# An adapter block whose token maxima change PSUM banks: from the pair of banks of the main maxima to a ring of three, in four units of two heads

## The chip, the cores and the metric

The kernel runs on one core of one Trainium2 chip. The metric is the time of one execution on the device, in microseconds (us); smaller is better. A profiled execution gives a trace of every instruction on the engines: PE (TensorE matmul) and PEld (its weight load), DVE (VectorE), ACT (ScalarE), POOL (GpSimd) and SP (which issues the transfers).

## The reference, cut to what matters

Three blocks follow one another on x (8 batches, 256 tokens, width 160) and a context (8 batches, 512 rows, width 96): a cross attention with an adapter branch, then a self attention, then a second cross attention with a feed-forward at the end. The change lies in the first. The context splits into 508 keys `enc` and 4 tokens `ca`:

```
query = x @ Wq;  hs = mha(query, enc @ Wk, enc @ Wv)            # 8 heads of 20
ca_q1 = einsum('btc,th->bch', ca, Wq_ca)[:, indices, :]         # 96 distinct rows out of 4 tokens
ca_hs1 = mha(ca_q1, x, x)                                       # 96 queries over 256 rows of x
ca_hs2 = mha(ca_hs1 @ Wq, ca @ Wk_ca, ca @ Wv_ca)               # over 4 keys
out = (hs + ca_hs2) @ Wout + b_out + x
```

The softmax of `ca_hs1` needs, for each of 96 queries and each of 8 heads, the maximum of its scores over the 256 rows of x. These are "the tokens' maxima over x".

## The kernel before, in words

The first block is one program of numbered **slots**, g = 0 to 38. A pair of heads p (four pairs in a batch, 32 in all) enters at slot p and passes on: its q and k are projected in slot p, its maxima found in slot p+2, turned ("mt") in slot p+3, its scores computed in slot p+4 and its output weighed in slot p+5 ("weigh", in four groups). A slot has two steps, 0 and 1; each engine walks the same list `items(g)` in the same order, so the order of work on every engine is written out by hand and each engine is first in, first out.

The work of a whole batch is spread over the slots by offsets: `add(step, what, offset)` puts a unit for batch b into slot 4b + offset. A period is thus four slots. I name them for batch b: slot **A** is 4b+1, **B** is 4b+2, **C** is 4b+3, **D** is 4b+4 (the slot in which the next batch begins its "rows").

PSUM has eight banks: two for the main maxima (`max_bank`), two for scores (`score_bank`), one for the weighed sums (`pv_bank`), and three `shared` ones, used as a ring. The class `Order` lists all the units that go through the ring in the order of the slots; unit number n uses bank n mod 3. TensorE fills a bank after `claim(key)`, which waits until the unit three places before has been read: by VectorE (semaphore `emptied`), or for "mt", "d1" and "e1" by ScalarE (`turned`). VectorE increments `emptied` in the order of the list, so a claim also waits for every earlier read of VectorE.

In `max_bank` two kinds of units alternate. `find_max` (L2091) does two matmuls per step of a pair, and VectorE reduces them (L1881). `top` (L2137) does four matmuls for four heads of the token scores, and VectorE reduces them (L1893) into `top_q`; there are two for a batch, at the ends of slots A and B. `find_max` of step 0 waits for `top_read` of the preceding `top`, and `top` waits for `max_read`. After both, "mq" (slot C, step 1) turns the maxima.

The units of the ring that the text names: "e3" (adapter branch, read by L1807 and L1809), "ot" (attention output turned, filled by L1965 and L1966, read by ScalarE and then L1775 and L1776), "out" 0 and 1 (output projection L1977, read by L1782), "x" (next batch's x turned, L1942 and L1943, read by ScalarE and then L1762, L1763), "q" and "k" (L2081, read by ScalarE and then L1754, L1758), "qw" (L2163), "ctx" (next batch's context turned, L1949, read by ScalarE L1666 and then VectorE L1767), "d1" (L1993), "v" (L1958), "rows" (L1985).

Of the kernel before, what the change touches and what calls it, by code (L numbers as in the profile page):

```python
# [15 lines left out]
AX = mybir.AxisListType  # L16
# [1273 lines left out]
def adapter(nc, x, x_dram, const, ident_tile, shapes, ctx_dram, l0, self_weights):  # L1290
# [33 lines left out]
    def items(g):  # L1324

        out = []

        def add(step, what, offset, *n):
            if (b := batch(g, offset)) is not None:
                out.append((step, (what, b, *n)))  # L1330

        add(0, "s2", 8)
        add(0, "v", 4, 1)
        add(0, "p2", 8)
        add(0, "e3", 9)
        add(0, "out", 10, 0)
        add(0, "out", 10, 1)
        if (b := batch(g, -1)):
            out.append((0, ("ctx", b)))
        add(0, "d1", 7)  # L1340
        if (p := pair(g, MT)) is not None:
            out.append((0, ("mt", p)))
        add(0, "ot", 9)
        if (b := batch(g, -2)):
            out.append((0, ("x", b)))
        if (p := pair(g, WEIGH)) is not None:
            out += [(0, ("weigh", p, group)) for group in (0, 1)]
        if (p := pair(g, 0)) is not None:
            out += [(1, ("q", p)), (1, ("k", p))]
        if g < 4:  # L1350
            out += [(1, key) for key in ([("w", 0), ("w", 1), ("ct",)], [("qk", n) for n in range(4)],
                                         [("g2",), ("vt",)], [("vo",)])[g]]
        add(1, "xv", 4)
        add(1, "qs", 4, 0)
        add(1, "qs", 5, 1)
        if (p := pair(g, WEIGH)) is not None:
            out += [(1, ("weigh", p, group)) for group in (2, 3)]
        add(1, "top", 1, 0)
        add(1, "top", 2, 1)
        add(1, "rows", 0)  # L1360
        add(1, "mq", 3)
        add(1, "d2", 7)
        add(1, "v", 3, 0)
        add(1, "e1", 8)
        add(1, "qw", 6)
        return out

    ELSEWHERE = ("weigh", "top", "qs", "s2", "p2", "xv")
    pre = [("ctx", 0), ("x", 0), ("wt",)]
    order = Order(pre + [key for g in range(SLOTS) for _, key in items(g) if key[0] not in ELSEWHERE], ("mt", "d1", "e1"))  # L1370

# [9 lines left out]
    with stack:  # L1381
# [127 lines left out]
        x_bo_ready = sem("x_bo_ready")  # L1509
        r_hi = sem("r_hi")  # L1510
        cm_ready = sem("cm_ready")
        top_filled = sem("top_filled")
        top_read = sem("top_read")
        q_scored = sem("q_scored")
        q_exped = sem("q_exped")
        q_split = sem("q_split")
# [216 lines left out]
        def _(dve):  # L1733
# [143 lines left out]
            def slot(g):  # L1877
                for step in range(ROUNDS):
                    if (p := pair(g, MAX)) is not None:
                        dve.wait_ge(max_filled, p * ROUNDS + step + 1)  # L1880
                        nc.vector.reduce_max(maxima[:, p % 2, step, :, 0], max_bank[:, :].rearrange("p (j k) -> p j k", j=2)[:, :, 0:KEYS],  # L1881
                                             AX.X).then_inc(max_read, 1)
                    for at, key in items(g):
                        if at != step or key[0] in ("weigh", "mt", "d1", "e1", "qs", "xv", "s2"):
                            continue
                        if key[0] in SETUP:
                            set_up(key)
                        elif key[0] == "p2":
                            second_softmax(key[1])
                        elif key[0] == "top":  # L1890
                            _, b, n = key
                            dve.wait_ge(top_filled, b * 2 + n + 1)
                            nc.vector.reduce_max(top_q[:, CDIM + 4 * n:CDIM + 4 * n + 4],  # L1893
                                                 max_bank[0:CDIM, :].rearrange("p (h k) -> p h k", h=4), AX.X).then_inc(top_read, 1)
                        else:
                            extra(key)
                if (p := pair(g, WEIGH)) is not None:
                    dve.wait_ge(pv_done, p + 1)
                    groups = pv_bank[:, 0:4 * AV]
                    nc.vector.reciprocal(recip[:, :], groups.rearrange("p (g d) -> p g d", d=AV)[:, :, AD]).then_inc(recip_ready, 1)  # L1900
                    dve.wait_ge(recip_ready, p + 1)
                    head = p % APAIRS * 2
                    out = attn[p // APAIRS % 2][:, :, head * AD:(head + 2) * AD].rearrange("p t (h d) -> p h t d", h=2)
                    nc.vector.tensor_tensor(out, groups.rearrange("p (h t d) -> p h t d", h=2, t=QT)[:, :, :, 0:AD],
                                            recip[:, :].rearrange("p (h t) -> p h t", h=2)[:, :, :, None].to_broadcast([P, 2, QT, AD]),
                                            ALU.mult).then_inc(attn_ready, 1)
# [13 lines left out]
        def _(pe):  # L1920
# [8 lines left out]
            def extra(key):  # L1929
# [48 lines left out]
                elif what == "rows":  # L1978
                    bank_ = claim(key)
                    if b == 0:  # L1980
                        pe.wait_ge(diag_ready, 3)
                    passes = [(diag_h[:, 0], x_h[j][:, 0, :]), (diag_h[:, 0], x_l[j][:, :]), (diag_l[:, :, :], x_h[j][:, 0, :]),
                              (diag_h[:, 1], x_h[j][:, 1, :])]
                    for n, (lhs, rhs) in enumerate(passes):
                        mm = nc.tensor.matmul(bank_[:, 0:SEQ], lhs.rearrange("p r c -> p (r c)"), rhs, start=n == 0, stop=n == 3)  # L1985
                elif what == "mq":
                    pe.wait_ge(top_read, b * 2 + 2)
                    bank_ = claim(key)
                    mm = nc.tensor.transpose(bank_[:, 0:CDIM], top_q[:, :], ident[0:CDIM, 0:CDIM])
                elif what == "d1":  # L1990
                    pe.wait_ge(emptied, order.read(("qw", b)))
                    bank_ = claim(key)
                    nc.tensor.transpose(bank_[:, 0:CDIM], hs1[:, 0:HA], ident[0:CDIM, 0:CDIM])  # L1993
                    mm = nc.tensor.transpose(bank_[0:HB, CDIM:2 * CDIM], hs1[:, HA:HID], ident[0:CDIM, 0:CDIM])
                elif what == "d2":
                    pe.wait_ge(turned, order.turned(("d1", b)))
                    bank_ = claim(key)
                    out = bank_[0:CDIM, 0:HT]
                    nc.tensor.matmul(out, hs1_t[:, 0, :], g2[:, 0, b, :], start=True, stop=False)
                    mm = nc.tensor.matmul(out, hs1_t[0:HB, 1, :], g2[0:HB, 1, b, :], start=False, stop=True)  # L2000
                elif what == "e1":
                    pe.wait_ge(p2_ready, b + 1)
                    bank_ = claim(key)
                    mm = nc.tensor.transpose(bank_[0:HT, 0:CDIM], p2n[:, :, :].rearrange("p h t -> p (h t)"), ident[0:CDIM, 0:CDIM])
                elif what == "e3":
                    pe.wait_ge(turned, order.turned(("e1", b)))
                    bank_ = claim(key)
                    rows = slice(b % 4 * HT, (b % 4 + 1) * HT)
                    mm = nc.tensor.matmul(bank_[0:CDIM, 0:HID], p2_t[rows, :], vo[rows, b // 4, :], start=True, stop=True)
# [74 lines left out]
            def find_max(g, step, p):  # L2084
                at = p % KEPT
                if step == 0:
                    pe.wait_ge(emptied, order.read(("k", p)))
                    after(pe, top_read, extra_fills(g, 1))
                after(pe, max_read, p * ROUNDS + step)
                for j, half in enumerate(HALF):  # L2090
                    mm = nc.tensor.matmul(max_bank[:, j * 512:j * 512 + KEYS], q_s[half, at, step * P:(step + 1) * P],  # L2091
                                          k_s[half, at, 0:KEYS], start=True, stop=True)
                mm.then_inc(max_filled, 1)
# [31 lines left out]
                if group == 3:  # L2125
                    mm.then_inc(pv_done, 1)

            def top(g, b, n):

                j = b % 2  # L2130
                if n == 0:
                    pe.wait_ge(emptied, order.read(("rows", b)))
                    pe.wait_ge(cm_ready, b + 1)
                after(pe, top_read, b * 2 + n)
                after(pe, max_read, issued(g, MAX))
                for h in range(4):
                    mm = nc.tensor.matmul(max_bank[0:CDIM, h * SEQ:(h + 1) * SEQ], c_m[j][0:3 * HT, 4 * n + h, :],  # L2137
                                          r_s[j][0:3 * HT, :], start=True, stop=True)
                mm.then_inc(top_filled, 1)

            def token_scores(g, b, t):

# [24 lines left out]
            def slot(g):  # L2167
                for step in range(ROUNDS):
# [4 lines left out]
                    for at, key in items(g):  # L2173
# [4 lines left out]
                        elif key[0] in ("q", "k"):  # L2178
                            project(key)
                        elif key[0] == "top":  # L2180
                            top(g, key[1], key[2])
                        elif key[0] == "qs":
                            token_scores(g, key[1], key[2])
                        elif key[0] == "qw":
# [54 lines left out]
```

## Time and profile before

| | us |
|---|---|
| three runs of the kernel | 1373.13, 1379.3, 1382.82; median 1379.3 |
| the profiled execution | 1376.87 |
| its span, from first to last instruction | 1375.0 |
| TensorE busy in it | 1272.2 (93%) |
| VectorE busy in it | 963.3 (70%) |

The profiled execution is 2.4 us below the median and 1.9 us longer than its span. The first block takes the first 307 us of the span, about a fifth. Busy time of TensorE is an upper bound of its real work, since matmuls are pipelined and their ends are modelled. The granted TensorE clock is given as a share of full speed (2.4 GHz); 0.50 is 1.2 GHz.

### The profile page before, as it was taken

Reading aid. Unit: us, or ns where it says so; the run is one execution under the profiler, and the core shown is the slowest. Engines: PE = TensorE matmul, PEld = TensorE weight load, DVE = VectorE, ACT = ScalarE, POOL = GpSimd, SP = SyncE. Lnnn points to the kernel's source line nnn. Section 1 sums busy time; section 2 is a strip of 40 time slices with the busy share of each in tenths; the row PEclk is TensorE's granted clock in tenths of the full one; section 3 lists DMA queues with packets and bytes.
Section 4 is the critical chain, followed back from the end, with each engine's and each line's share of the span. In section 5 each row is a group of like instructions: output and inputs, shape, how many; then the busy total and the mean of one; then the engine's idle time right before and its main releaser. Section 6 shows DMA issues by size and latency. Waiting matters only on the chain. (4 is left out here: it accounts for less than half of the span.)

```text
span 1375.0 us, 39629 instructions
## 1 busy us (share of the span) xinstructions
PE 1272.2 (93%) x16812; PEld 1084.5 (79%) x16812; DVE 963.3 (70%) x1758; ACT 779.5 (57%) x1420; POOL 810.6 (59%) x866
## 2 busy tenths in 40 slices
PE   4889999976999999999889999999999999999597
PEld 3677777755989989899757888888888888887597
DVE  4677887734777777777457767686867676765584
ACT  2366666644656665665346656565656665655364
POOL 2278887657645655555426656566656565667364
PEclk9999999957999999999969999999999999999798
DMA  6001110002000000000010000000010000000000
GB/s 133 21 11 50 50 35 2 2 7 65 2 2 2 2 3 2 2 2 2 1 42 8 2 8 2 8 2 8 1 49 2 2 2 2 2 2 2 13 15 25
DMA packets 31992, 20.40 MB, mean 15 GB/s; under 512 B 21415, under 2 KB 30347, under 8 KB 31819
## 3 DMA queue, kind: packets, MB, share of 16 engines
q1 hardware_dynamic: 31819, 17.88, 5.2%
q8 instruction: 135, 2.21, 0.7%
q14 instruction: 38, 0.31, 0.1%
HBM read 16.56 MB, written 1.31 MB: 13 GB/s over the span
## 5 line engine op out<-in xcount | busy, mean ns | idle before, releaser
L530 POOL TENSOR_TENSOR cross_probs_l<-cross_probs 128x1024 f16<-128x1024 f32 x160 | 302.6, 1893 | 54.6 <-ACT cross_probs L614 54.6
L614 ACT ACTIVATE cross_probs<-cross_score 128x1024 f32<-128x1024 f32 x160 | 163.9, 1024 | 189.4 <-PE cross_score L844 189.4
L698 DVE TENSOR_REDUCE cross_top<-cross_max 128x2 f32<-128x1024 f32 x160 | 195.7, 1223 | 63.6 <-PE cross_max L818 63.6
L1618 POOL TENSOR_TENSOR ad_probs_l<-ad_probs 128x1024 f16<-128x1024 f32 x64 | 120.8, 1893 | 91.2 <-ACT ad_probs L1692 90.8
L530 POOL TENSOR_TENSOR self_probs_l<-self_probs 128x1024 f16<-128x1024 f32 x80 | 151.4, 1892 | 1.2 <-ACT self_probs L614 1.2
L864 PEld LDWEIGHTS cross_pv<-cross_v_h,cross_probs 128*128 128x128 bf16 x1280 | 117.1, 98 | 38.0 <-issue 26.8
L614 ACT ACTIVATE self_probs<-self_score 128x1024 f32<-128x1024 f32 x80 | 81.9, 1024 | 110.9 <-PE self_score L844 110.8
L864 PE MATMUL cross_pv<-cross_v_h,cross_probs 128*128 128x65 bf16 x1280 | 135.7, 196 | 6.1 <-POOL cross_probs_l L530 5.3
L865 PE MATMUL cross_pv<-cross_v_l,cross_probs 128*128 128x64 f16 x1280 | 134.4, 194 | 0.0
L866 PE MATMUL cross_pv<-cross_v_h,cross_probs_l 128*128 128x65 bf16 x1280 | 134.0, 194 | 0.0
L844 PE MATMUL cross_score<-cross_qk_h 64*128 64x256 f32 x640 | 120.5, 373 | 0.0
L865 PEld LDWEIGHTS cross_pv<-cross_v_l,cross_probs 128*128 128x128 bf16 x1280 | 118.8, 99 | 0.2
L866 PEld LDWEIGHTS cross_pv<-cross_v_h,cross_probs_l 128*128 128x128 f16 x1280 | 118.7, 99 | 0.0
L684 DVE TENSOR_TENSOR cross_qk_l<-cross_shared,cross_qk_h 128x256 fp32r<-128x256 f32 (+1 forms) x160 | 88.0, 553 | 32.8 <-ACT cross_qk_h L599 32.6
L698 DVE TENSOR_REDUCE self_top<-self_max 128x4 f32<-128x1024 f32 x80 | 97.7, 1222 | 17.9 <-PE self_max L823 17.7
L511 POOL CAST cross_maxima<-cross_top 128x4 bf16<-128x4 f32 x80 | 16.0, 200 | 151.3 <-DVE cross_top L698 151.3
L511 POOL CAST self_maxima<-self_top 128x4 bf16<-128x4 f32 x80 | 16.1, 202 | 136.1 <-DVE self_top L698 136.0
L1692 ACT ACTIVATE ad_probs<-ad_score 128x1024 f32<-128x1024 f32 x64 | 65.5, 1024 | 52.5 <-PE ad_score L2103 51.8
L599 ACT CAST cross_qk_h<-cross_shared 128x256 fp32r<-128x256 f32 (+1 forms) x160 | 76.1, 477 | 26.7 <-PE cross_shared L800 23.9
L844 PE MATMUL cross_score<-cross_qk_l,cross_qk_h 64*128 64x256 f32 x640 | 90.3, 279 | 0.0
L844 PE MATMUL cross_score<-cross_qk_h,cross_qk_l 64*128 64x256 f32 x640 | 90.2, 278 | 0.0
L684 DVE TENSOR_TENSOR self_qk_l<-self_shared,self_qk_h 128x512 fp32r<-128x512 f32 x80 | 55.2, 690 | 42.8 <-ACT self_qk_h L599 42.6
(438 smaller groups left out, 4792.4 us busy)
## 6 DMA issues: line engine op xcount, KB each, us to landing
ad_ctx_rows<-in_ctx SPq DMA_DIRECT2D x8, 192.0 KB, 2.8
cross_ctx_rows<-in_ctx SPq DMA_DIRECT2D x8, 192.0 KB, 2.6
sw_raw<-in_L_xattn_wq SPq DMA_DIRECT2D x2, 640.0 KB, 6.1
sw_raw<-in_L_xattn_wk SPq DMA_DIRECT2D x2, 640.0 KB, 4.8
sw_raw<-in_L_xattn_wv SPq DMA_DIRECT2D x2, 640.0 KB, 5.2
cw_raw<-in_L_xattn_wq SPq DMA_DIRECT2D x2, 640.0 KB, 4.2
lr_raw<-in_L_xattn_w_ff SPq DMA_DIRECT2D x2, 640.0 KB
out<-x_rows SPq DMA_DIRECT2D x8, 160.0 KB, 1.9
```

The source lines that it names most:

```text
L511: nc.gpsimd.tensor_copy(maxima[:, p % 2, :, :, 0], top[:, p % 2, :, :]).then_inc(max_hi, 1)
L530: nc.gpsimd.tensor_tensor(probs_l[:, n % PR, :, :].rearrange("p j k -> p (j k)"), whole, whole.bitcast(BF16)[:, 1::2], ALU.subtract).then_ ...
L599: nc.scalar.copy(qk_h[:, kept(parity, s), at:at + width], shared[ring.bank(kind, key)][:, 0:width]).then_inc(qk_hi, 1)
L614: nc.scalar.activation(probs[:, n % PR, :, :].rearrange("p j k -> p (j k)"), score_bank[:, :], ACT.Exp, scale=SCALE).then_inc(exped, 1)
L684: nc.vector.tensor_tensor(qk_l[:, kept(parity, s), at:at + width], shared[ring.bank(kind, key)][:, 0:width], qk_h[:, kept(parity, s), at:a ...
L698: nc.vector.reduce_max(out, scores, AX.X).then_inc(max_read, 1)
L844: mm = nc.tensor.matmul(score_bank[:, j * 512 + c * SEQ:j * 512 + (c + 1) * SEQ], ks[half, at, keys], qs[half, at, 0:SEQ], start=False, st ...
L864: nc.tensor.matmul(pv_bank[:, at:at + DV], hi, v_h[parity][:, c, head, :], start=c == 0, stop=False)
L865: nc.tensor.matmul(pv_bank[:, at:at + DH], hi, v_l[parity][:, c, head, :], start=False, stop=False)
L866: mm = nc.tensor.matmul(pv_bank[:, at:at + DV], lo, v_h[parity][:, c, head, :], start=False, stop=last)
L1618: nc.gpsimd.tensor_tensor(probs_l[:, n % PR, :, :].rearrange("p j k -> p (j k)"), whole, whole.bitcast(BF16)[:, 1::2], ALU.subtract).then_ ...
L1692: nc.scalar.activation(probs[:, n % PR, :, :].rearrange("p j k -> p (j k)"), score_bank[:, :], ACT.Exp, scale=SCALE).then_inc(exped, 1)
```

## The change: what it does

The tokens' maxima no longer use `max_bank`. They become four units of two heads each (n = 0 to 3), which go through the ring of three shared banks: n = 0 in slot A, step 0, behind "ot"; n = 1 in slot A, step 1, where `top` 0 stood; n = 2 in slot B, step 1, where `top` 1 stood; n = 3 in slot C, step 0, behind "mt". I call them T0 to T3. The two semaphores `top_filled` and `top_read` go; `find_max` no longer waits for a token unit, and the token units no longer wait for `max_read`. They claim a ring bank instead. "mq" waits for the read of T3.

```diff
         add(0, "ot", 9)
+        add(0, "top", 1, 0)
+        add(0, "top", 3, 3)
         if (b := batch(g, -2)):
             out.append((0, ("x", b)))
...
-        add(1, "top", 1, 0)
-        add(1, "top", 2, 1)
+        add(1, "top", 1, 1)
+        add(1, "top", 2, 2)
...
-    ELSEWHERE = ("weigh", "top", "qs", "s2", "p2", "xv")
+    ELSEWHERE = ("weigh", "qs", "s2", "p2", "xv")
...
# VectorE
-                            dve.wait_ge(top_filled, b * 2 + n + 1)
-                            nc.vector.reduce_max(top_q[:, CDIM + 4 * n:CDIM + 4 * n + 4],
-                                                 max_bank[0:CDIM, :].rearrange("p (h k) -> p h k", h=4), AX.X).then_inc(top_read, 1)
+                            dve.wait_ge(filled, order.filled(key))
+                            nc.vector.reduce_max(top_q[:, CDIM + 2 * n:CDIM + 2 * n + 2],
+                                                 shared[order.bank(key)][0:CDIM, :].rearrange("p (h k) -> p h k", h=2), AX.X).then_inc(emptied, 1)
...
# TensorE, "mq"
-                    pe.wait_ge(top_read, b * 2 + 2)
+                    pe.wait_ge(emptied, order.read(("top", b, 3)))
...
# TensorE, find_max
                     pe.wait_ge(emptied, order.read(("k", p)))
-                    after(pe, top_read, extra_fills(g, 1))
                 after(pe, max_read, p * ROUNDS + step)
...
# TensorE, top
-            def top(g, b, n):
+            def top(b, n):
...
-                after(pe, top_read, b * 2 + n)
-                after(pe, max_read, issued(g, MAX))
-                for h in range(4):
-                    mm = nc.tensor.matmul(max_bank[0:CDIM, h * SEQ:(h + 1) * SEQ], c_m[j][0:3 * HT, 4 * n + h, :],
+                bank_ = claim(("top", b, n))
+                for h in two:
+                    mm = nc.tensor.matmul(bank_[0:CDIM, h * SEQ:(h + 1) * SEQ], c_m[j][0:3 * HT, 2 * n + h, :],
                                           r_s[j][0:3 * HT, :], start=True, stop=True)
-                mm.then_inc(top_filled, 1)
+                mm.then_inc(filled, 1)
```

## Rows read from the trace of the kernel before

**Rows 1.** The page: busy time, share and instructions of each engine.

```profile
PE 1272.2 (93%) x16812; PEld 1084.5 (79%) x16812; DVE 963.3 (70%) x1758; ACT 779.5 (57%) x1420; POOL 810.6 (59%) x866
```

**Rows 2.** Windows, slot A to A: length; busy PE, PEld, DVE, ACT, POOL; clock.

```profile
94.39:125.48 31.09, 28.18 (x388) 23.63 (x388) 24.90 (x46) 21.75 (x42) 26.70 (x16) 0.95 0.18 49
...
217.06:248.41 31.35, 28.29 (x388) 23.61 (x387) 24.90 (x46) 20.85 (x41) 24.12 (x15) 0.95 0.01 2
```

**Rows 3.** Windows, slots A, B, C, D of batch 4.

```profile
155.87:163.72 7.85, 6.41 (x83) 4.85 (x83) 7.17 (x14) 5.79 (x12) 7.85 (x7) 1.00 0.37 125
163.72:172.74 9.02, 8.78 (x137) 7.88 (x138) 6.41 (x11) 5.36 (x8) 7.23 (x5) 0.81 0.06 22
172.74:179.58 6.84, 6.54 (x86) 5.49 (x87) 5.76 (x10) 4.24 (x9) 6.76 (x4) 1.00 0.24 50
179.58:185.91 6.33, 6.18 (x83) 5.08 (x83) 5.81 (x14) 5.37 (x11) 3.79 (x3) 1.00 0.01 3
```

**Rows 4.** Timeline of TensorE at the ends of slots A and B.

```profile
161.59 0.68 PE L2137 MATMUL ad_max<-ad_r_s,ad_c_m 96*96 96x256 f32 x4
163.72 0.50 PE L2091 MATMUL ad_max<-ad_k_s,ad_q_s 64*128 64x508 f32 x2 [1.45 <-issue]
...
170.59 0.69 PE L2137 MATMUL ad_max<-ad_r_s,ad_c_m 96*96 96x256 f32 x4
171.12 0.19 PE L2163 MATMUL ad_shared<-ad_xv_h,ad_probs_q 128*128 128x21 bf16 x1
...
172.74 0.50 PE L2091 MATMUL ad_max<-ad_k_s,ad_q_s 64*128 64x508 f32 x2 [0.24 <-issue]
```

**Rows 5.** Timeline of VectorE, slots A to C.

```profile
158.57 0.32 DVE L1809 TENSOR_TENSOR ad_branch_l<-ad_shared,ad_branch_h 96x160 f16<-96x160 f32 x1
...
159.78 0.41 DVE L1776 TENSOR_TENSOR ad_attn_ts<-ad_shared,ad_attn_ts 32x256 fp32r<-32x256 f32 x1
...
162.40 1.21 DVE L1893 TENSOR_REDUCE ad_top_q<-ad_max 96x4 f32<-96x1024 f32 x1
...
165.39 0.32 DVE L1782 TENSOR_TENSOR x_rows<-ad_shared,x_rows 128x160 f32<-128x160 f32 x1
...
175.03 0.69 DVE L1767 TENSOR_TENSOR ad_ctx_l<-ad_shared,ad_ctx_h 96x512 fp32r<-96x512 f32 x1 [0.44 <-ACT ad_ctx_h L1666]
```

**Rows 6.** Windows of TensorE alone: the last of seven idle stretches behind L2137.

```profile
254.81:256.25 1.44, 0.00 (x0) 1.00 0.00 0
```

**Rows 7.** Windows: the half-clock stretches of batches 1 and 7.

```profile
72.70:79.50 6.80, 6.80 (x72) 5.79 (x71) 3.93 (x6) 4.19 (x7) 5.21 (x4) 0.50 0.00 0
...
257.20:263.80 6.60, 6.60 (x66) 5.57 (x64) 3.16 (x5) 3.23 (x6) 3.44 (x2) 0.50 0.00 0
```

**Rows 8.** DVE groups by form, 30 to 300 us: two reductions.

```profile
L1893 DVE TENSOR_REDUCE ad_top_q<-ad_max 96x4 f32<-96x1024 f32 x16 | 19.4, 1215 | 1.3 <-PE ad_max L2137 1.2
...
L1795 DVE TENSOR_REDUCE ad_top<-ad_shared 96x8 f32<-96x32 f32 x8 | 1.5, 188 | 3.5 <-PE ad_shared L2000 3.3
```

**Rows 9.** Timeline of TensorE around the places of T0 and T3.

```profile
157.87 0.19 PE L2122 MATMUL ad_pv<-ad_v_h,ad_probs 128*128 128x21 bf16 x1
...
166.18 0.42 PE L1942 MATMUL ad_shared<-shape_consts,x_rows 128*128 128x128 f32 x1
...
174.27 0.17 PE L2122 MATMUL ad_pv<-ad_v_h,ad_probs 128*128 128x21 bf16 x1
...
178.67 0.39 PE L1958 MATMUL ad_shared<-ad_wv_h,ad_ctx_h 96*128 96x256 f32 x1 [0.20 <-DVE ad_k_s L1758]
```

**Rows 10.** Windows around two other idle stretches of TensorE, and behind them.

```profile
274.10:277.40 3.30, 1.95 (x35) 1.57 (x33) 3.23 (x6) 2.66 (x7) 2.28 (x2) 1.00 0.02 5
277.60:280.90 3.30, 3.30 (x37) 2.43 (x37) 2.03 (x5) 2.06 (x3) 3.30 (x3) 0.50 0.00 0
...
1257.10:1260.50 3.40, 2.22 (x42) 1.78 (x41) 1.23 (x1) 1.11 (x3) 3.16 (x2) 1.00 0.00 0
1260.60:1263.90 3.30, 2.63 (x46) 2.15 (x44) 1.74 (x3) 2.02 (x3) 1.86 (x3) 1.00 0.01 2
```

More of the change, by code:

```diff
@@ L1511, in adapter @@
         cm_ready = sem("cm_ready")
-        top_filled = sem("top_filled")
-        top_read = sem("top_read")
         q_scored = sem("q_scored")
@@ L2180, in slot @@
                         elif key[0] == "top":
-                            top(g, key[1], key[2])
+                            top(key[1], key[2])
                         elif key[0] == "qs":
```

## The prediction

> **What bounds the kernel now.** I read the page first: TensorE is busy 93% of the span, VectorE 70% [rows 1]. The share says little of the place of the change, so I cut the first block into its periods. In the five batches 2 to 6 a period from slot A to slot A takes 30.0 to 31.4 us; TensorE is busy 28 of them, VectorE 25 [rows 2]. TensorE sets the pace with VectorE close behind it. Next I cut one period into its four slots [rows 3]. Slot A holds 1.44 us in which TensorE does nothing (7.85 less 6.41). Slot B runs at a mean clock of 0.81: the clock is halved in part of it, and (1 - 0.81) x 9.02 = 1.7 us of TensorE's time are lost to that.
>
> The timeline of TensorE shows where both come from [rows 4]. Behind the token unit L2137 at the end of slot A it idles 1.45 us before `find_max`, which waits until VectorE has read the token unit: that read runs from 162.40 for 1.21 us [rows 5], to 163.61, and `find_max` starts at 163.72, so a semaphore takes about 0.1 us. The same stretch is there in all seven batches from 1 to 7 (1.36 to 1.45 us; the last of them in [rows 6]), and behind each the clock falls to 0.50, 1.2 GHz, within about a microsecond: for some 3.4 us in batches 2 to 6, for twice that in batches 1 and 7 [rows 7]. The second token unit, at the end of slot B, has "qw" between it and the next `find_max` and costs only 0.24 us of idle time [rows 4]. So the structure that the change takes away costs, per batch, 1.45 + 0.24 us of waiting and 1.7 us of slow clock.
>
> **What the change removes, step by step.** Slot A: from the start of L2137 to `find_max` are 2.13 us [rows 4]. T1 stands there instead, with half the matmuls. Four matmuls of `top` cost TensorE 0.53 us (170.59 to 171.12 [rows 4]), so two cost 0.27. Nothing then waits for a token read: -1.86 us. Slot B: T2 for the second unit, -0.27, and the wait of 0.24 goes: -0.5. T0 in A and T3 in C bring the matmuls back, +0.27 each. TensorE's own work is unchanged, eight matmuls a batch.
>
> VectorE: a reduction of 1024 elements takes 1.215 us, one of 32 takes 0.188 [rows 8]; on the line between them one of 512 takes 0.69. Four of these for two long ones are 2.74 for 2.43, +0.3 us a batch. VectorE has 5 to 6 us free in a period [rows 2]; I take it at zero on the path and 0.3 as its upper bound. Nothing changes for ScalarE, GpSimd or the transfers. "mq" waits for T3's read, which ends some 2 us before "mq" is due: zero.
>
> **What it adds: claims in a ring.** I wrote out the ring in the new order; each unit claims the bank of the unit three places before:
>
> A: e3 mt ot **T0** | q k **T1**; B: out0 out1 mt x | q k **T2** qw; C: ctx d1 mt **T3** | q k mq d2 v; D: v mt | q k rows e1.
>
> Two of the claims are late.
>
> *T0 claims the bank of e3*, which is the first unit VectorE reads in slot A, after the first reduction of the main maxima. Its read ends at 158.57 + 0.32 = 158.89 [rows 5]. TensorE would come to T0 at about 157.75, since the next instruction, the first weighing, starts at 157.87 behind a short wait of its own [rows 9]. So T0 starts at 158.99, and the weighing at 159.26 instead of 157.87: +1.39 us, with 1.2 us of idle time. Queued behind T0 on TensorE are the weighing groups, the second `find_max` and score, q and k: all are 1.4 us late, and ScalarE and GpSimd with them. k now claims ot's bank, read at 159.78 + 0.41 = 160.19 [rows 5]; k would come at about 161.2, so that costs nothing. Net for slot A: -1.86 + 1.39 = -0.5 us.
>
> *T3 claims the bank of ctx*, read by ScalarE and then VectorE. That read ends at 175.03 + 0.69 = 175.72 [rows 5], 2.98 us after the start of slot C at 172.74 [rows 4]. TensorE is ready for T3 at 174.27, where the weighing starts now [rows 9]. The chain to the read (fill, exponential on ScalarE, ctx on ScalarE, then VectorE) starts from TensorE's own work in slot C, so it moves along with the slot: a wait of 1.45 + 0.1 = 1.55 us, and 0.27 for the matmuls: +1.8 us. It buys back about 0.15: q had waited for the same read of ctx. Net for slot C: +1.7 us. The bounds are +1.3 (if VectorE, relieved of the long reduction, reaches ctx 0.4 earlier) and +2.1.
>
> *x claims the bank of out0* as before, but now this may bind. The main reduction and out0 stand behind T1's read on VectorE. That read starts between 162.40 (as L1893 did [rows 5]) and 163.8; I take 163.4, since k is 1.4 us late and VectorE had been 0.4 behind k. From there to the end of out0's read were 3.3 us (162.40 to 165.71 [rows 5]), of which 0.5 go with the shorter reduction and 0.3 were a wait for TensorE: out0's bank is free at about 165.95. TensorE, with B starting at 163.25, would be there 1.85 us later (166.18 - 163.72 less 0.6 us of slow clock [rows 9]), at 165.1: a wait of 0.85 us, between 0 and 1.2. At full clock slot B changes by -0.5 - 1.7 + 0.85, plus some 0.5 because half of the 1.7 had lain over waits for x's chain anyway: -0.9 us.
>
> **The sum at full clock** for batches 2 to 6: -0.5 - 0.9 + 1.7 = +0.3 us a batch.
>
> **The clock decides the rest.** Idle stretches of 1.45 us behind L2137 were followed by the half clock every time. Around 1.2 us it went both ways: in one stretch TensorE idled 3.30 - 1.95 = 1.35 us and the clock fell behind it, in another 3.40 - 2.22 = 1.18 and it stayed [rows 10]. T3's wait (1.55) is nearest to the first kind, T0's (1.2) to the last. I take 0.8 of a half-clock stretch a batch, mostly behind T3, at 1.7 us each: +1.4. Batches 2 to 6: 5 x (0.3 + 1.4) = +8.5 us.
>
> The Trainium skill, "TensorE: Matmul & The Clock Gate", section "A second HAM failure mode: psum-queue depth-cycling", says that a kernel which cycles through PSUM banks can idle so often in small pieces that the clock swings between its two levels, and loses its throughput to that. It speaks against this change, which lengthens the cycle through the ring. The trace agrees as to the kind of loss (1.7 us per stretch in slot B); by that rule the third rival below would be the forecast.
>
> The other batches: batch 1 has no e3 yet, so T0 is free: -1.6; slot B -0.5, and its half clock lasted twice as long [rows 7], about -2.9; slot C +1.7; one new half clock at 0.8, +1.4. Sum -1.9. Batch 7 has e3 but no ctx behind it: A -0.5, B -0.5, its long half clock -2.6, T3's matmuls +0.3, a half clock in some executions +0.3: -3.0. Batch 0 loses two waits of 1.4 but gets T3's and, in slot A, one for "rows": about 0, between -2 and +1. The self attention, the cross attention and the feed-forward don't use these banks: 0.
>
> Total: +8.5 - 1.9 - 3.0 - 0.2 = **+3.4 us**, 1380.3 against the profiled execution's 1376.87 and 1382.7, rounded to **1383**, against the median of 1379.3.
>
> **The rivals.** (1) *The half clock goes altogether*: if neither new wait brings it, batches 2 to 6 lose the 1.4 and batch 1 too: 3.4 - 7.0 - 1.4 = -5, 1374. For it: stretches of 1.2 to 1.35 us that were borderline. Against it: 1.55 is longer than any that got by.
> (2) *The waits are hidden and the gain is whole*: per batch 1.6 + 0.24 us of waiting and 1.7 of clock, 3.5 x 8 = 28 us, 1351. This needs e3 and ctx read before TensorE comes to T0 and T3; both reads hang on TensorE's own start of the slot, and VectorE's long reduction stands ahead of e3, so little speaks for it.
> (3) *Slower: two half-clock stretches a batch.* Mechanism: TensorE now idles 1.2 us in slot A and 1.55 in slot C; if both bring the half clock, batches 2 to 6 pay 0.3 + 3.4 = 3.7 each, 18.5, and batches 1 and 7 another 2: with -4.9 - 0.2 from above +15.5, 1395. It decides from where T0's wait acts like the 1.35 us stretch of [rows 10] rather than the 1.18 one, or where x's and T0's waits fall close together.
> (4) *The change doesn't do what it says*, that is, `find_max` still waits for VectorE: its reduction of step 1 must be read before step 0 of the next slot. That read ends before T1 is issued, so I give this 0.03 and put it with the forecast's time plus 5.
>
> **How the numbers follow.** Forecast 0.53 (own range 1377 to 1390), rival 1 0.17, rival 2 0.07, rival 3 0.20, rival 4 0.03. About 1% (14 us) is what a measurement of this kernel can tell from no change: its three runs lie 10 us apart. Faster by over 1% is rival 2 and a little: 0.08. Slower by over 1% (above 1393) takes two thirds of rival 3 and a tail of the forecast, where T3's wait is at its upper bound: 0.20. Within 1%: 0.72. The range runs from 1369 (rival 1 with T3's lower bound) to 1397 (rival 3); it leaves out rival 2 and the top of rival 3.
>
> **What the changed profile would show.** TensorE's idle stretch before L2091 of slot B gone; a new one of about 1.2 us before T0, released by VectorE L1809, in batches 2 to 7; one of about 1.5 us before T3, released by VectorE L1767, in batches 0 to 6; one of up to 1 us before x. Token reductions of about 0.69 us, 32 of them. The half clock moved from slot B to behind T3, into slots C and D. The period of batches 2 to 6 between 31 and 33 us. I am wrong if T3's wait is under 0.5 us, if the weighing behind it proves to have been waiting for something else, or if the clock stays at 1.00 through a whole period.

## The result, and the profile after

| | before | after |
|---|---|---|
| first measurement, median (us) | 1378.9 (4 runs) | 1395.7 (1383.9 to 1398.3, 4 runs) |
| ratio, 95% interval | | 1.0115 [1.0081, 1.0149] |
| the kernel after once more, on the chip of the last experiments (us) | 1374.0 (19 runs) | 1388.8 (1379.2 to 1393.7, 4 runs) |
| ratio, 95% interval | | 1.0101 [1.0057, 1.0144] |
| profiled execution / its span (us) | 1376.87 / 1375.0 | 1393.85 / 1392.0 |

The change makes the kernel 1.0 to 1.2% slower, 15 to 17 us, and both intervals lie wholly above 1. The forecast of 1383 had the sign; the time is that of the third rival. TensorE's row of the page, to be read against [rows 1]:

```profile
PE 1284.6 (92%) x16812; PEld 1090.6 (78%) x16812; DVE 969.4 (70%) x1774; ACT 780.6 (56%) x1420; POOL 810.8 (58%) x866
```

As many matmuls take 12.4 us more; VectorE has 16 instructions and 6.1 us more. The first block ends at 319.2 us where it ended at 306.9. The windows of batches 2 to 6 in the kernel after, slot A to slot A (length; busy PE, PEld, DVE, ACT, POOL; clock), against [rows 2]:

```profile
94.77:125.39 30.62, 26.82 (x387) 21.92 (x386) 25.02 (x48) 21.73 (x42) 26.64 (x16) 1.00 0.19 55
125.39:161.59 36.20, 33.07 (x387) 27.24 (x386) 25.64 (x48) 22.32 (x42) 27.51 (x18) 0.76 0.12 33
161.59:193.26 31.67, 28.10 (x387) 22.76 (x386) 25.27 (x48) 20.86 (x40) 22.98 (x13) 0.95 0.12 29
193.26:224.85 31.59, 28.09 (x387) 22.94 (x386) 25.20 (x48) 20.87 (x41) 23.81 (x15) 0.95 0.10 28
224.85:261.38 36.53, 33.40 (x388) 27.50 (x387) 25.15 (x48) 21.45 (x41) 24.84 (x16) 0.77 0.01 2
```

These five take 166.6 us, before 154.0. Read the length and the clock together: a period at full clock takes 30.62, two with clocks of 0.76 and 0.77 take over 36. The period at full clock (batch 2) by slots A to D, against those of batch 4 in [rows 3]:

```profile
94.77:102.29 7.52, 6.38 (x82) 4.83 (x81) 5.73 (x12) 6.71 (x14) 7.30 (x6) 1.00 0.01 2
102.29:110.57 8.28, 7.35 (x137) 6.37 (x136) 6.76 (x13) 5.42 (x9) 8.20 (x6) 1.00 0.01 2
110.57:119.08 8.51, 6.94 (x93) 5.63 (x90) 6.73 (x11) 4.24 (x9) 7.40 (x4) 1.00 0.50 130
119.08:125.39 6.31, 6.16 (x83) 5.08 (x82) 5.80 (x14) 5.36 (x11) 3.73 (x2) 1.00 0.24 87
```

Slot A is 0.33 shorter than before, B 0.74 shorter, C 1.67 longer, D the same. TensorE's timeline shows the three waits, T0, x and T3 of batch 6, against [rows 9]; the releaser in brackets is the read of the bank claimed (e3, out0, ctx):

```profile
228.03 0.45 PE L2135 MATMUL ad_shared<-ad_r_s,ad_c_m 96*96 96x256 f32 x2 [1.14 <-DVE ad_branch_l L1809]
...
236.47 0.30 PE L1942 MATMUL ad_shared<-shape_consts,x_rows 128*128 128x128 f32 x1 [0.65 <-DVE x_rows L1782]
...
244.84 0.48 PE L2135 MATMUL ad_shared<-ad_r_s,ad_c_m 96*96 96x256 f32 x2 [1.34 <-DVE ad_ctx_l L1767]
```

T0's wait is there in batches 2 to 7 (1.14 each time), T3's in batches 1 to 6 (1.34 or 1.35), x's in batches 2 to 6 (0.64 to 0.93); the wait before L2091 of [rows 4] is gone. The token reductions, by form, against [rows 8]:

```profile
L1893 DVE TENSOR_REDUCE ad_top_q<-ad_shared 96x2 f32<-96x512 f32 x32 | 21.9, 684 | 5.0 <-PE ad_shared L2135 4.8
```

And the clock behind one T0 (its wait ends at 128.58) and one T3 (145.25):

```profile
127.40:130.10 2.70, 1.56 (x33) 1.40 (x32) 2.20 (x6) 1.38 (x5) 2.05 (x2) 1.00 0.02 6
130.30:133.50 3.20, 3.20 (x22) 2.62 (x20) 1.86 (x4) 2.08 (x4) 1.89 (x1) 0.50 0.00 0
133.70:147.20 13.50, 11.51 (x198) 9.66 (x195) 10.54 (x21) 8.29 (x16) 12.21 (x7) 1.00 0.12 26
147.40:160.80 13.40, 13.40 (x119) 11.14 (x117) 8.70 (x17) 7.79 (x15) 8.55 (x5) 0.50 0.16 53
```

Between 60 and 275 us the kernel before has 31 us of half clock in seven stretches, the kernel after 48 us in seven: four begin within 2.3 us behind a T0 (17 us in all), three within 2.1 us behind a T3 (31 us in all, with two stretches of 13.7 us among them). How much half clock there is differs from execution to execution. The second profile of the kernel after is that of the fastest of its four executions; its batches 4 and 6:

```profile
155.73:186.04 30.31, 26.80 (x387) 21.86 (x386) 25.60 (x49) 20.74 (x40) 25.68 (x16) 1.00 0.17 49
...
217.61:250.61 33.00, 29.45 (x387) 24.05 (x387) 25.17 (x48) 21.05 (x41) 24.11 (x15) 0.90 0.01 2
```

It has 17 us of half clock there, in four stretches, three behind a T0 and one behind a T3; its five periods take 156.2 us, and its span is 1377.3. The waits are the same to 0.02 us. In the first measurement the four executions at mean clocks of 0.955, 0.944, 0.937 and 0.936 took 1383.9, 1393.9, 1398.3 and 1397.6 us.

### The profile page after: what moved, and what is told of

Read it like the earlier page. It is cut to its first block and busy times, and to the rows that moved or that the text cites. A ratio compares the mean times of both kernels' runs of the same rounds, so it can differ in the third digit from the quotient of the medians.

```text
span 1392.0 us, 39629 instructions
## 1 busy us (share of the span) xinstructions
PE 1284.6 (92%) x16812; PEld 1090.6 (78%) x16812; DVE 969.4 (70%) x1774; ACT 780.6 (56%) x1420; POOL 810.8 (58%) x866
## 5 line engine op out<-in xcount | busy, mean ns | idle before, releaser
L599 ACT CAST cross_qk_h<-cross_shared 128x256 fp32r<-128x256 f32 (+1 forms) x160 | 76.1, 477 | 26.8 <-PE cross_shared L800 23.9
```

What stands on the lines that cost most here:

```text
L599: nc.scalar.copy(qk_h[:, kept(parity, s), at:at + width], shared[ring.bank(kind, key)][:, 0:width]).then_inc(qk_hi, 1)
```

## The experiments

Theory W: TensorE's waits for the reads of e3 and ctx, ahead of T0 and T3, are what costs, with the half clock that they bring. The rivals were that the ring is late everywhere, that only the waits count, or only the clock. "First set" had before at 1375.1 (25 runs), "second set" at 1376.9 (25 runs), "third set" at 1374.0 (19 runs).

### First set: T3 moved alone

```diff
-        add(0, "top", 3, 3)
...
         add(1, "qw", 6)
+        add(1, "top", 2, 3)
```

> The changed kernel with T3 moved alone: from slot C, step 0 (where it claims the bank of ctx) to slot B, step 1, behind qw, where it claims the bank of k. Theory W (the loss is in two waits, T0 on the read of e3 and T3 on the read of ctx, and in the half clock that they bring): the wait of 1.35 us before T3 goes in seven batches, 9.5 us, and with it part of the half clock, 3 to 8 us: 1378 to 1384 against the changed kernel's 1396 and 1379 before. No idle stretch of TensorE over 0.5 us in slot C. Rival R (four more units make the ring late everywhere, and a unit moved away leaves its wait to the next claim): ctx, d1 or mt now wait as long as T3 did, and the time stays at 1390 or more.

Measured: 1371.5 us, ratio 0.9962 [0.9940, 0.9983]: 0.4% faster than the kernel before, and 6.5 us below the range expected. Two of its periods, batches 4 and 6:

```profile
147.94:177.04 29.10, 26.72 (x387) 21.90 (x387) 25.42 (x49) 20.75 (x40) 25.66 (x16) 1.00 0.17 52
...
206.67:239.01 32.34, 30.62 (x388) 25.33 (x388) 25.19 (x48) 21.05 (x41) 24.14 (x15) 0.84 0.01 2
```

No wait over 0.5 us is left in slot C, so rival R falls: ctx, d1 and mt don't inherit it. T0 still waits 1.14 us in all six batches, and only that of batch 6 is followed by the half clock, 10 us of it. The five periods take 150.0 us for 166.6. At full clock a period is 1.2 us shorter (29.38 for batch 2, 30.62 in the kernel after), 6 us for five; the other 10 are clock, by the first profile of the kernel after. Against its second profile (156.2) the whole gain is 6.2 us, so what moving T3 gives back in clock depends on the execution compared with.

### First set: T0 moved alone

```diff
-        add(0, "top", 1, 0)
...
+        add(1, "top", 1, 0)
         add(1, "top", 1, 1)
```

> The changed kernel with T0 moved alone: from slot A, step 0 (where it claims the bank of e3) to slot A, step 1, directly ahead of T1, where it claims the bank of ot; T3 stays in slot C. Theory W: the wait of 1.15 us before T0 goes in six batches, 6.9 us; but out0 and x now stand behind two token reads on VectorE, so the wait of x in slot B grows from 0.65 to about 1.6 us and takes most of it back: 1388 to 1394, T3's wait of 1.35 us unchanged. Rival R (the wait is a matter of the ring's length): the same 1390 to 1396, but with the wait before q or k of slot A. Rival S (T0's wait is the one that brings most of the half clock): 1380 or less.

Measured: 1394.7 us, ratio 1.0138 [1.0075, 1.0201]. T0 no longer waits. x of slot B waits 1.24 in place of 0.65, less than the 1.6 expected:

```profile
169.95 0.30 PE L1942 MATMUL ad_shared<-shape_consts,x_rows 128*128 128x128 f32 x1 [1.24 <-DVE x_rows L1782]
```

Two token reads now stand ahead of out0's on VectorE. The time is just above the range, since the half clock stayed (58 us of it between 60 and 275 us). T3 of batch 3 and TensorE's clock around and behind it:

```profile
143.78 0.48 PE L2135 MATMUL ad_shared<-ad_r_s,ad_c_m 96*96 96x256 f32 x2 [1.35 <-DVE ad_ctx_l L1767]
...
142.30:145.40 3.10, 1.75 (x34) 1.40 (x32) 2.04 (x4) 1.57 (x6) 2.28 (x2) 1.00 0.41 88
145.60:159.00 13.40, 13.40 (x98) 11.14 (x99) 8.49 (x16) 7.65 (x14) 7.97 (x4) 0.50 0.17 50
```

T3 waits 1.34 or 1.35 us in batches 1 to 5, and the half clock begins 1.3 to 2.0 us behind it in four of the five, batches 2 to 5, for 44 of the 58 us; the other three stretches begin 1.4 to 2.2 us behind x's wait. So rival S falls: the half clock does not need T0's wait. Rival R falls too, since no wait over 0.5 us stands before q or k of slot A.

### First set: matmuls in the waits, after and before

The added matmuls fill TensorE's waits; their results are never read.

```diff
+            def fill(g, count):
+                if (p := pair(g, WEIGH)) is None:
+                    return
+                after(pe, attn_ready, p)
+                for _ in range(count):
+                    nc.tensor.matmul(pv_bank[:, 0:SEQ], fill_w[:, :], fill_rows[:, :], start=True, stop=True)
...
+                if n in FILLS:           # {0: 9, 3: 11, "x": 5}; the same ahead of extra(("x", b))
+                    fill(g, FILLS[n])
```

> The changed kernel with matmuls that nobody reads put ahead of T0 (9), T3 (11) and x (5), each 128 by 256 in bf16 into the bank of the weighed sums, which is free then; they compute nothing that is used, and last about as long as TensorE idles there (1.0, 1.2 and 0.5 us). The waits stay as they are; only TensorE is busy in them. Theory C (a good half of the loss is slow clock, brought by the idle stretches): the half clock of 48 us in all between 60 and 285 us is nearly gone, which gives back up to 20 us: 1374 to 1382. Rival W1 (the loss is the waits themselves and the half clock lies over waits anyway): 1390 to 1400, with the clock at 1.00 and periods as long as in the changed kernel.

Measured: 1375.4 us, ratio 0.9982 [0.9960, 1.0005]. The same 12 matmuls of that size in the kernel before, into `score_bank`, ahead of the wait for `top_read`:

> The kernel before with 12 such matmuls that nobody reads ahead of the find_max of slot B, into the bank of the scores, in the 1.45 us in which TensorE waits for VectorE's read of the token unit; nothing else changed. Theory C: the wait stays, the half clock of 3.4 us (6.8 in batches 1 and 7) goes in seven batches: 1.7 x 7 + 3 = 15 us at most, 1364 to 1370. Rival W1: within 3 us of the kernel before, 1376 to 1382, although the clock stays at 1.00.

Measured: 1366.8 us, ratio 0.9932 [0.9908, 0.9956]. Batch 4 of the filled kernel after, then of the filled kernel before:

```profile
157.70:188.01 30.31, 29.53 (x412) 24.24 (x411) 25.62 (x49) 20.73 (x40) 25.68 (x16) 1.00 0.17 50
```

```profile
151.94:180.90 28.96, 28.09 (x401) 23.08 (x400) 25.07 (x47) 20.75 (x40) 25.63 (x16) 1.00 0.18 53
```

No half clock is left between 64 and 265 us in either. Theory C holds for the kernel after: by the ratios (1.0101 or 1.0115 less 0.9982) 16 to 18 us come back from busy matmuls that do nothing. In the kernel before it is 8 to 9 us, in the range expected for the time (1364 to 1370) but well under the 15 us named as the most: the half clock costs it 5.9 us in batches 2 to 6 (154.0 less 148.2), 1.2 a stretch and not 1.7. The two filled kernels also price the waits by themselves: 153.4 us against 148.2 for five batches, +1.05 us a batch at full clock. Of the 12.6 us that the first profile loses in these batches, the new waits are 5.3 and the clock the other 7.3 (13.2 for the 5.9 of the kernel before).

### Second set: the same ring, T0 and T3 later in TensorE's queue

```diff
-        add(0, "top", 1, 0)
-        add(0, "top", 3, 3)
...
             out += [(0, ("weigh", p, group)) for group in (0, 1)]
+        add(0, "top", 1, 0)
+        add(0, "top", 3, 3)
```

> The changed kernel with its ring exactly as it is, but T0 and T3 issued by TensorE behind the first two weighing groups of their slots. Theory W: T0's wait falls from 1.15 to 0.5 us, T3's from 1.35 to 0.7, 8 us in all, and the half clock that both had brought goes for the most part, another 8 to 10 us: 1376 to 1382. Rival R (it is the place in the ring that costs, not the place in TensorE's queue): 1388 to 1396, with find_max of step 1 or q late by as much as before.

Measured: 1367.8 us, ratio 0.9946 [0.9925, 0.9967], 8 us below the range expected. T0 and T3 of batch 4 in this kernel (T0 waits 0.55 in the others):

```profile
157.01 0.33 PE L2135 MATMUL ad_shared<-ad_r_s,ad_c_m 96*96 96x256 f32 x1 [0.39 <-DVE ad_branch_l L1809]
...
171.90 0.36 PE L2135 MATMUL ad_shared<-ad_r_s,ad_c_m 96*96 96x256 f32 x1 [0.77 <-DVE ad_ctx_l L1767]
```

The claims are those of the change and VectorE's order is unchanged; only 0.6 us of weighing was let past each wait. Against the kernel after that is 20 us or more, and 6.8 us of half clock are left in its profile. So it is not the place in the ring that costs but what is queued on TensorE behind the claim.

### Second set: the best placements found

T3 behind "qw" and T0 behind the weighing (the two edits above, one each):

> T3 behind qw in slot B, as in the experiment before, and T0 kept in its place in the ring (it claims the bank of e3) but issued by TensorE behind the first two weighing groups of slot A instead of ahead of them. Theory W (T0's cost is that the weighing is queued behind its wait): the weighing takes 0.65 us, so T0's wait falls from 1.14 to about 0.5 us in six batches, 3 to 4 us, and no half clock follows it: 1364 to 1370 where T3 behind qw alone gave 1371.5. Rival (x is the next to wait: slot B starts earlier, out0's read doesn't): x's wait grows from 0.65 to 1.0 or more and the time stays within 2 us of 1371.5.

Measured: 1366.9 us, ratio 0.9928 [0.9907, 0.9949]; x waits 0.72 to 1.12 us, with T3 moved alone 0.64 to 1.11. The rival wanted 1.0 or more and a time within 2 us of 1371.5; the first is met in two batches, where T3 moved alone has one, and the time is not (ratios 0.9928 and 0.9962). One half clock of 6.8 us was left where none was expected. Then also x ahead of out0 and out1:

```diff
-        add(0, "out", 10, 0)
-        add(0, "out", 10, 1)
...
         if (b := batch(g, -2)):
             out.append((0, ("x", b)))
+        add(0, "out", 10, 0)
+        add(0, "out", 10, 1)
```

> The kernel of t3_qw_t0_weigh with x moved ahead of out0 and out1 in slot B, on all engines: x then claims the bank of k, out0 that of T1 and q that of x. Theory W (x's wait for out0's read is the third cost of the ring, 0.65 to 0.95 us in six batches): x doesn't wait, out0 waits less than 0.3 us for T1's read: 4 to 6 us less than t3_qw_t0_weigh, 1360 to 1366. Rival V (VectorE sets the pace by now, and a wait of TensorE taken away comes back at the next reduction): within 2 us of t3_qw_t0_weigh, with the wait before out0 or before find_max of step 1.

Measured: 1361.2 us (6 runs), ratio 0.9890 [0.9865, 0.9915], the fastest of all kernels here. Batches 4 and 6:

```profile
151.20:179.53 28.33, 26.89 (x387) 21.90 (x386) 25.17 (x49) 20.66 (x40) 25.59 (x16) 1.00 0.18 55
...
208.53:237.56 29.03, 26.94 (x387) 22.17 (x386) 24.83 (x48) 20.75 (x41) 24.09 (x15) 1.00 0.01 2
```

What is left in these periods are waits of 0.4 to 0.55 us before T0 and before k of slot A, and one before out1 (0.76 once, else 0.45), whose bank ScalarE's L1657 frees; there is no half clock up to 263 us. Five periods take 144.1 us, 10 fewer than before. Theory W holds: x no longer waits, and the time is in its range. Rival V falls, since 5.6 us came off where it allowed 2.

### Second set: both moves of the first set

> T3 behind qw in slot B and T0 in slot A, step 1, ahead of T1 (the two moves of the first set together). Theory W with what the first set showed (T0 in step 1 takes its wait of 1.15 away but raises that of x to 1.25): no wait of T0 or T3, x waits 1.25 us in six batches and brings a half clock now and then: 1368 to 1378, no better than T3 behind qw alone at 1371.5. Rival (the two moves add up, since T3 had pushed x late): 1362 to 1367.

Measured: 1366.6 us (1357.2 to 1379.2), ratio 0.9923 [0.9899, 0.9946]. x waits 1.24 in batches 2 to 6 as with T0 moved alone, which was the theory's; the median is better than its range and in the rival's. The half clock, in one profile, came once for 24 us, behind x's wait of batch 6; behind the same wait in batches 2 to 5 it did not come:

```profile
151.65:180.23 28.58, 26.75 (x387) 21.79 (x386) 25.16 (x49) 20.78 (x40) 25.62 (x16) 1.00 0.18 54
...
209.87:247.32 37.45, 35.29 (x388) 28.80 (x388) 24.96 (x48) 21.48 (x41) 25.03 (x17) 0.68 0.01 2
```

### Third set: which wait brings the half clock

The filled kernel after with `FILLS = {0: 9, 3: 0, "x": 0}`, then with `{0: 0, 3: 11, "x": 0}`, and the kernel after itself.

> The changed kernel with matmuls that nobody reads ahead of T0 alone (9 of 128 by 256 in bf16, into the free bank of the weighed sums). The question is which wait brings the half clock. Theory T3 (the longer wait, 1.35 us, brings it by itself, as 1.45 us did in the kernel before): a stretch of half clock behind T3 in most of its seven batches stays, some 24 to 30 us in all of 48: 1384 to 1390. Theory SUM (no wait does it alone; T0's 1.15, T3's 1.35 and x's 0.65 do it together): under 12 us of half clock, 1376 to 1381.

> The same ahead of T3 alone (11 such matmuls). Theory T3: as T3 behind qw, 10 us of half clock, since T0's 1.15 us seldom brings it: 1376 to 1382. Theory T0 (T0's wait, with x's 10 us behind it, is what brings it): 30 us or more of half clock, 1386 or more. Theory SUM: under 12 us, 1376 to 1381.

> The changed kernel itself, unchanged, beside the other two on one chip: 1388 to 1400, with 35 us or more of half clock between 60 and 275 us, at other places than in the first profile.

| filled | median (us) | ratio | half clock, 60 to 275 us |
|---|---|---|---|
| T0 alone | 1374.8 | 0.9997 [0.9975, 1.0019] | 0 |
| T3 alone | 1383.1 | 1.0043 [1.0018, 1.0068] | 37 us in five stretches |
| none | 1388.8 | 1.0101 [1.0057, 1.0144] | 17 us in four |

T3 of batch 4 and the period of batch 4 with T0 filled:

```profile
176.07 0.44 PE L2149 MATMUL ad_shared<-ad_r_s,ad_c_m 96*96 96x256 f32 x2 [1.44 <-DVE ad_ctx_l L1772]
...
157.43:187.84 30.41, 27.80 (x398) 22.76 (x397) 25.60 (x49) 20.77 (x40) 25.71 (x16) 1.00 0.16 48
```

T0 of batch 4 and the period with T3 filled:

```profile
159.12 0.33 PE L2149 MATMUL ad_shared<-ad_r_s,ad_c_m 96*96 96x256 f32 x1 [1.14 <-DVE ad_branch_l L1814]
...
155.97:189.53 33.56, 31.90 (x398) 26.36 (x397) 25.83 (x49) 20.96 (x40) 25.73 (x16) 0.85 0.15 45
```

Theory T3 falls: with T0 filled, six waits of 1.44 us, the longest in the period, brought no half clock in the profile. With T3 filled, T0's 1.14 us were followed by it five times in six, as theory T0 said; the time, 1383, is between the theories. Theory SUM falls with the 37 us. For the kernel after itself the 35 us or more of half clock that were expected did not come either; it was 17.

Which wait brings the half clock is not settled by this. With T0's wait gone (T0 moved alone) T3's 1.35 us were followed by it four times in five. With T3's wait gone, T0's 1.14 us were followed by it five times in six where T3 was filled and once in six where T3 was moved, although the waits left are the same two, T0's and x's. And one of the ten executions with T0 filled took 1403.8 us at a mean clock of 0.936, the other nine 1370.4 to 1380.7 at 0.961 to 0.969; no trace of it was kept. What the runs do show is that filling all three waits takes the half clock away, and that with T0's filled alone nine executions of ten are as fast as with all three.

## Why the prediction came out as it did

**The waits were read rightly.** T0: 1.2 forecast, 1.14 measured, released by the read of e3. T3: 1.55 forecast, 1.34 or 1.35 measured, released by the read of ctx. x: 0.85 forecast, 0.64 to 0.93. Token reductions: 0.69 forecast, 0.684. At full clock the forecast made slot A 7.4 us long, B 8.1, C 8.5 and D 6.3; the first full-clock period has 7.52, 8.28, 8.51 and 6.31. The sum "+0.3 us a batch" made batch 4 last 30.3 us; it is 30.31 in the second profile. Over the five batches the filled kernel has -0.6 us for the +1.5 forecast. These are claims read off the order of the ring and the ends of VectorE's reads, and nothing else was needed.

**The term that was mis-sized is the clock**: "I take 0.8 of a half-clock stretch a batch, mostly behind T3, at 1.7 us each: +1.4", 7.0 us for batches 2 to 6, 8.5 with the waits. The first profile has +12.6 us there (166.6 less 154.0), of which -0.6 lies in the full-clock part (153.4, the filled kernel, less 154.0) and 13.2 in the clock, 2.6 a batch; the second has 2.8 in the clock, 0.6 a batch. So the forecast of 7.0 us lies between two executions of the same kernel, and the medians stand nearer to the first. There were six stretches in batches 2 to 6 of the first profile for the four forecast, and their length was off most: 13.7 us in two of them, for 3.4 in the kernel before. The place was half right: in the first profile 31 of the 48 us lie behind a T3, as forecast, but T0's wait, taken as the harmless one, is followed by the half clock four times in six, and three times in six in the second profile. The step that failed is "nearest in length", and its reading of [rows 10] was wrong too. The 1.35 us there are the idle time of a whole window, whose longest wait is 1.21; in the other window, behind which the clock stayed, it is 1.18:

```profile
277.08 0.58 PE L2149 MATMUL ad_score<-ad_c_m,ad_r_s 128*128 128x384 f32 x2 [1.21 <-ACT ad_probs L1692]
...
1258.47 0.20 PE L864 MATMUL cross_pv<-cross_v_h,cross_probs 128*128 128x65 bf16 x1 [1.18 <-POOL cross_probs_l L530]
```

So waits of about 1.2 us had gone both ways, and the rows gave no ground for taking T0's 1.2 us as harmless.

**The price of a stretch of half clock** in slot B of the kernel before was right: 1.7 us less 0.5 that lay over waits, and filling its wait gives back 1.2 a batch.

**The other batches**: the "-0.2" in the total has no source in the working. Batch 1 -2.3 (forecast -1.9), batch 7 -0.7 (-3.0, its 6.8 us of half clock stayed), the set-up before slot A of batch 1 +2.7 (about 0, between -2 and +1; 0.91 of it is T0's wait for "rows"). The later blocks took 4.7 us more in the first profile, though none of their instructions changed; in the second profile 0.8 more. What of the 4.7 is due to the phase of the clock in them was not isolated.

**The rivals.** The first (no half clock) was priced 5 us below the kernel before; with the waits filled the ratio of 0.9982 makes it 2.5, and the interval reaches the time of the kernel before. The third (1395) has the time that was measured. Its mechanism, both waits bringing the half clock, is what the first profile shows, four times behind T0 and three behind T3, but with six stretches in batches 2 to 6 for its ten, two of them four times as long as it had them, and 4.7 us from the later blocks that it put at nothing: that its total fits is in part luck. Its condition, that T0's wait acts like the stretch before the fall in [rows 10], was met in more than half of the batches. It deserved more than 0.20, and the forecast's place within 1% less than 0.72. Rival 2 fell with the waits, rival 4 with the missing wait before `find_max`.

The Trainium skill, "TensorE: Matmul & The Clock Gate", section "A second HAM failure mode: psum-queue depth-cycling", describes the kind of loss that decided: a cycle through PSUM banks with idle pieces between the groups makes the clock swing. The trace agrees, with 48 us of half clock for 31 in the first profile; the second, with 17, shows that it does not do so in every execution, and the kernel with x ahead, which cycles through the same three banks with waits of at most 0.76 us in batches 2 to 6, has none.

## What to carry to other kernels

When a unit is moved into a shared ring of banks, write out who claims whose bank and ask which engine's last instruction frees it; then ask what stands behind the claim in the filling engine's queue, and let 0.6 us of ready work past it before moving anything else. A wait of 1.1 to 1.4 us before a claim may cost several times its length through the clock (two of T3's were followed by 13.7 us at half clock), so price an idle stretch of TensorE twice, once as waiting and once as half clock, with the second as a wide range: for the same five batches of the same kernel it was 2.8 us in one execution and 13.2 in another. Idle matmuls ahead of a wait are a cheap test of which of the two it is.

## What the runs showed of the hardware

- The half clock does not follow from the length of the idle stretch before it. In the kernel before, 1.36 to 1.45 us behind L2137 were followed by it seven times in seven; in the kernel with T0 filled, 1.44 us ahead of T3 were followed by it in none of six, and in the kernel with T0 moved 1.34 or 1.35 us ahead of T3 four times in five. A stretch of 1.14 us ahead of T0 was followed by it once in six with T3 moved, and five times in six with T3 filled. What distinguishes them stays open. The seven in the kernel before are no seven independent trials: they begin 30.7 us apart each time, while the periods last 30.0 to 31.4.
- Once fallen, the clock stayed at 0.50 for 3.4, 6.8, 10.2 or 13.7 us in these periods, once for 23.9 (both moved), and in the kernel after, from 147.4 to 160.8 us, TensorE was busy for all of it (13.40 of 13.40) without the clock coming back sooner. Why some stretches last four times as long as others was not tried.
- Matmuls whose results nobody reads, 12 of 128 by 256 in bf16 in each wait of some 1.45 us, made the kernel before 0.7% faster.
